# The weight tiles of a cross-attention kernel moved by 32 bytes

## What is computed

```python
text_p  = x   @ W_text  + b_text          # 512 -> 512
audio_p = ctx @ W_audio + b_audio         # 384 -> 512
Q = layer_norm(text_p, g1, beta1)
K = layer_norm(audio_p, g2, beta2)
alpha = softmax(Q @ K.T / sqrt(512))      # 256 x 256 in each sequence
h = (alpha @ audio_p) @ W_out + b_out
out = layer_norm(h + x, g_out, beta_out)
```

## Time and profile before

| | |
|---|---|
| median of 3 runs | 1266.14 us (1266.1 to 1266.36) |
| profiled execution: its time | 1266.2 us |
| profiled execution: its span, first to last instruction | 1264.4 us |
| TensorE matmuls | 1251.3 us busy, 6648 of them |
| TensorE weight loads | 1067.3 us busy |
| VectorE, ScalarE, GpSimd | 1079.9, 1054.0, 548.7 us busy |
| TensorE's clock over the span | 0.999 of full speed |

### The profile page before, as it was taken

One profiled execution on the slowest core, in us unless ns is written; L12 is line 12 of the kernel. 1 busy time (PEld: TensorE's weight loads), 2 busy tenths in 40 slices (PEclk: granted clock), 3 DMA queues, 4 the chain that ended last, 5 costly groups with the idle time before them and its releaser, 6 DMA issues.

```text
span 1264.4 us, 22572 instructions
## 1 busy us (share of the span) xinstructions
PE 1251.3 (99%) x6648; PEld 1067.3 (84%) x6648; DVE 1079.9 (85%) x1735; ACT 1054.0 (83%) x1791; POOL 548.7 (43%) x545
## 2 busy tenths in 40 slices
PE   8999999999999999999999999999999999999997
PEld 6688888888888888888888888888888888888886
DVE  6788888898888888888988888888888888889888
ACT  7788888888888888888888888988888888888884
POOL 0122555433554434554435544335544345543356
PEclk9999999999999999999999999999999999999999
DMA  7356876777866767866768767678667688667693
GB/s 258 92 153 177 245 227 169 200 185 215 241 213 174 196 187 233 234 192 179 187 203 243 227 172 197 185 220 240 206 177 190 192 238 230 187 185 188 207 236 106
DMA packets 96645, 252.49 MB, mean 200 GB/s; under 512 B 9456, under 2 KB 25328, under 8 KB 88688
## 3 DMA queue, kind: packets, MB, share of 16 engines
q1 hardware_dynamic: 75408, 187.22, 42.2%
q0 software_dynamic: 21216, 65.02, 28.6%
HBM read 137.38 MB, written 49.81 MB: 148 GB/s over the span
## 4 chain that ended last, share of the span: by engine, by line
PE 97%; DVE 1%; ACT 1%; issue 0%; DMA 0%; SPq 0%; DVEq 0%; ACTq 0%
PE wide L372 9%; PE wide L376 9%; PE wide L375 9%; PE score L300 7%; PE score L301 7%; PE score L302 7%; PE wide L302 7%; PE wide L300 7%; PE wide L301 7%; PE wide L430 7%; PE wide L429 7%; PE wide L428 7%; PE turn L301 1%; PE turn L302 1%; PE turn L300 1%; PE turn L382 1%
## 5 line engine op out<-in xcount | busy, mean ns | idle before, releaser
L1275 POOL TENSOR_TENSOR y_rows<-y_rows,betao_row 128x512 f32<-128x512 f32 x120 | 166.7, 1389 | 339.3 <-ACT y_rows L649 226.3
L372 PE MATMUL wide<-xT_hi,wt_hi 128*128 128x512 f32 x496 | 195.8, 395 | 0.3 <-DVE xT_lo L860 0.3
L376 PE MATMUL wide<-xT_hi,wt_lo 128*128 128x512 f32 x496 | 195.9, 395 | 0.0
L375 PE MATMUL wide<-xT_lo,wt_hi 128*128 128x512 f32 x496 | 195.8, 395 | 0.0
L608 ACT ACTIVATE squares<-wide,bac_col 128x512 f32<-128x512 f32 x128 | 88.4, 690 | 78.8 <-PE wide L302 77.1
L302 PE MATMUL wide<-cT_hi,wa_lo 128*128 128x512 f32 x372 | 146.8, 395 | 0.0
L300 PE MATMUL wide<-cT_hi,wa_hi 128*128 128x512 f32 x372 | 146.8, 395 | 0.0
L430 PE MATMUL wide<-wao_hi,pcT_lo 128*128 128x512 f32 x372 | 146.7, 394 | 0.0
L428 PE MATMUL wide<-wao_hi,pcT_hi 128*128 128x512 f32 x372 | 146.6, 394 | 0.0
L301 PE MATMUL wide<-cT_lo,wa_hi 128*128 128x512 f32 x372 | 146.6, 394 | 0.0
L300 PE MATMUL score<-kT_hi,qT_hi 128*128 128x256 f32 x512 | 145.4, 284 | 1.1 <-DVE qT_lo L936 1.1
(11 more groups left out here) (170 smaller groups left out, 3554.0 us busy)
## 6 DMA issues: line engine op xcount, KB each, us to landing
xT_in<-in_xT SPq DMA_DIRECT2D x31, 1024.0 KB, 8.6
y_rows<-in_x_rows SPq DMA_DIRECT2D x124, 256.0 KB, 4.1
y_rows<-bao_row POOLq DMA_DIRECT2D x31, 1024.0 KB, 9.4
out<-y_rows SPq DMA_DIRECT2D x124, 256.0 KB, 3.4
xT_lo<-xT_in POOLq DMA_DIRECT2D x30, 1024.0 KB, 9.0
c_kept<-in_c_rows SPq DMA_DIRECT2D x32, 768.0 KB, 6.9
cT_in<-in_cT SPq DMA_DIRECT2D x31, 768.0 KB, 8.8
p_out<-probs SPq DMA_DIRECT2D x31, 512.0 KB, 4.7
```

The costliest lines, as they stand in the source:

```text
L372: nc.tensor.matmul(wide[h][:], wt_hi[:, d, cols], xT_hi[:, d, :], start=(d == 0), stop=False)
L375: nc.tensor.matmul(wide[h][:], wt_hi[:, d, cols], xT_lo[:, d, :], start=False, stop=False)
L376: done = nc.tensor.matmul(wide[h][:], wt_lo[:, d, cols], xT_hi[:, d, :], start=False, stop=(d == DT - 1))
L1275: nc.gpsimd.tensor_tensor(rows, rows, betao_row[:], ALU.add).then_inc(y_ready, 1)
```

## The change

A tile `line_fill` of 8 float32 a partition, 32 bytes, is declared ahead of the weights, and `b_shift`, behind the small tiles, is 32 bytes shorter. Everything declared between the two lies 32 bytes further: the six tiles of weights, the three rows (`bao_row`, `go_row`, `betao_row`), `cols` and the small tiles. What is declared ahead of them and behind them stays where it is. No instruction is added, removed or moved.

```diff
         mean_of = sb("mean_of", [P, P], F32R)
         eps = sb("eps", [P, 1])
 
+        line_fill = sb("line_fill", [P, 8])
+
         wt_hi, wt_lo = sb("wt_hi", [P, DT, H], F32R), sb("wt_lo", [P, DT, H], F32R)
         wa_hi, wa_lo = sb("wa_hi", [P, CT, H], F32R), sb("wa_lo", [P, CT, H], F32R)
         wao_hi, wao_lo = sb("wao_hi", [P, CT, H], F32R), sb("wao_lo", [P, CT, H], F32R)
@@
         b_sum, b_mean = sb("b_sum", [P, 2]), sb("b_mean", [P, 2])
 
-        b_shift = sb("b_shift", [P, 24])
+        b_shift = sb("b_shift", [P, 16])
 
         xT_in, cT_in = sb("xT_in", [P, DT, T * P]), sb("cT_in", [P, CT, T * P])
```

## The result

| | before | after |
|---|---|---|
| median | 1266.12 us | 1271.09 us |
| ratio, 95% interval | | 1.004 [1.003, 1.005] |
| span of the profiled execution | 1264.4 us | 1269.0 us |

The change makes the kernel 5.0 us slower, 0.4%. The forecast was no change, 1266.0 us. First the page and TensorE's waits after the change.

What follows compares the result with a forecast made beforehand. TensorE, busy almost throughout, was taken as the bound: matmuls times pitch. Profiled execution 1266.2 us, with loads 0, streams -0.2 and rest 0, gave 1265.9 to 1266.1, stated as 1266.0; the 8-in-10 range was 1257 to 1274 us.

Steps and rivals of the forecast that it cites:

- What bounds it: Whole kernel: TensorE is 99% busy with no waits from 60 to 1211 us, so time is matmuls times pitch.
- the cost of the stationary operands: 2688 weight loads, phase 0 under streams at phase 32: bounded at 0 to 20 ns each, taken as 0.
- The moving operands: Output stage, 1152 matmuls streaming wao: one 64-byte block fewer each, 0.2 us gain in all, at most 7.7.
- The bound from the context stage: Context streams touch 24 blocks, scores 17; seven more cost 1.5 ns, so 0.2 ns a block.
- Rival A: Output stage: 64-byte blocks feed the stream at about 7.04 ns each; 8.1 us less, 1258 us; chance 0.13.
- Wrong in another way: Sign of other failure: a new mid-kernel TensorE wait, or context and scores changing though their operands keep their addresses; no size.
- The rhythm of seven: Key stage: four matmuls of 0.39 us, then three of 0.40, repeating; read as excess not sitting on one operand.
- Rival C: Load and stream disturb each other when phases differ: 1293 us at 10 ns a load, 1274 at 3; chance 0.15.
- Rival B: Wide matmuls: phase makes the excess over streaming time, in loads and streams; 72.6 us less if all went, 1194; chance 0.05.
- the 18.9 ns: Each wide matmul's pitch beyond the 213.3 ns that 512 columns take at 2.4 GHz; whether addresses touch it was the question.
- the 16.4 ns: Wide matmul pitch, 232.2 ns, less the skill page's 215.8: unexplained, estimated at 63 us over 3840 matmuls, 1203 us.

Runs made afterwards that it cites:

- distance 0: Against the kernel before, weights 32 bytes nearer, data 96 further: stationary and moving addresses equal within 256 bytes; 1250.56 us. Weights 64 nearer, data 64 further: 1250.14 us.

## Why the prediction was wrong

**What bounds it** was right: TensorE's pitch, and nothing else. No wait appeared in the middle, and with the three rows and cols alone on 64 the time was that of before. The measured 1271.09 us also lies within the stated 1257 to 1274; but the forecast was 1266.0 us, with 0.67 on no change and 0.15 on slower.

**The step that failed** is the cost of the stationary operands: "So a load from phase 0 under a stream at phase 32 costs 0 to 20 ns ... I take 0: the output stage's reading is clean". I chose the lower end of a bound that I had rightly drawn, on the reading of a single mean_of load among 37 matmuls, read to 10 ns. The true cost was about 0.04 us / 36 = 1.1 ns a load in the keys and 0.03 / 48 = 0.6 in the queries, some 2 us in all. One load in a stage could not show 1 ns. Nor was it a reading of the change: by the declarations mean_of lay at distance 96 from `sq_parts` and `xT_hi` and at 224 from `wao_hi`, while keys and queries went to 160; that mean_of has phase 0 was the one thing they shared. And in the query stage the load of mean_of had also to wait for `sq_parts`: in the step of the earlier trace rows VectorE finished it at 600.59 us and the load began at 600.64, 0.08 us after the start of the matmul that it should lie behind.

**The moving operands** were the second miss, and the larger: forecast 0.2 us of gain, measured 0.07 us x 31 = 2.2 us of loss. The bound from the context stage answered how many blocks of 64 bytes a stream touches; that question was the wrong one. Rival A, which asked the same question from the other side, forecast 8 us of gain in the output stage and is refuted by the sign. Its agreement at 7.04 ns a block was chance: at distance 0 the streams touch 32 blocks in one kernel and 33 in the other, and the key stage takes 8.19 us in both.

**Context and scores** had no term in the sum, and grew by 0.8 us in 31 steps with operands that kept their addresses. The prediction named this under "Wrong in another way", as a sign "that the pitch hangs on something between tiles"; it is the smallest of the three parts, and no run explains it.

**The rhythm of seven** I read as proof that the excess does not sit on addresses. In that kernel it sits on no single operand, that was right; but the rhythm itself depends on the distance of the two operands. The same view of the changed kernel shows a pattern of three, with some 6 ns more after each L303, and at distance 0 the three members of the key triple have 226.9 to 227.7 ns on average. A rhythm out of step with the program says nothing on whether addresses set its mean.

**Rival C** came nearest, with a chance of 0.15: the position of the stationary operand against the moving one costs time. Its point of decision, 1 ns a load, is about where the keys came out. It counted phases within 64 bytes, where 64 bytes further is 7 us faster; it left the output stage out; its prices of 3 and 10 ns were too high; and that a load and the stream beside it are what meets, as it has it, no run shows. Rival B is refuted as stated (all at phase 0 is no faster), yet its reservation, that the rows could not separate the excess from the common position, was sound: of the 18.9 ns above 213.3, distance 0 removes 4.7.

**On the pages.** The Trainium skill, "TensorE: Matmul & The Clock Gate", section "Step-by-step: what each phase is for", has weights and moving operand on two independent read ports. The pitch of the same matmuls runs from 227.5 to 234.2 ns with the distance of those two operands alone, so here the two operands are not independent in time; whether it is their reads of SBUF that meet, no run shows. "SBUF — State Buffer", section "Door 1: The DMA port swizzle", gives lines of 16 bytes; a step of 16 bytes, from one such line to the next, took the key stage from 8.19 to 8.40 us. The gap of 215.8 ns, which "Back-to-back issue gap" gives for a matmul by itself, is not reached by the wide stages of any kernel; for a stream of loads and matmuls of 512 columns the section gives some 131 ns, far below the 226.8 ns that is the least in the map. So the 16.4 ns of rival B were measured against a figure that the section does not give for such a stream.

**What stays open**: whether the next load meets the running stream or a matmul's own operands meet, and what has a period of 256 bytes. The map is measured; what in the hardware makes it is not shown.

## What to carry to other kernels

In this kernel, where TensorE is busy to the end, the position of the stationary tile against the moving one is worth up to 3% of a wide matmul's pitch in this form of float32; other types and widths were not tried. Where the same holds, try the same position within 256 bytes first (1.2% of this kernel, 1250.14 us, for one line of declarations moved and a filler resized), and measure each position by itself, since neighbouring values do not interpolate. Before relying on one odd instruction as the witness for a thousand others, work out how small an effect per instruction it could show; if that is larger than the effect that decides, keep the bound and not its end.

## What the runs showed that I had not expected

Distance 0 is the best and 16 bytes from it is nearly the worst; of ten distances two are fast (0 and 192), and the others lie within 3 ns. In the kernel at distance 0 the matmul of the mean of squares was itself out of line in the query stage:

```profile
517.22 0.39 PE L372 MATMUL wide<-xT_hi,wt_hi 128*128 128x512 f32 x1
517.44 0.45 PE L382 MATMUL turn<-sq_parts,mean_of 128*128 128x512 f32 x1
517.73 0.39 PE L375 MATMUL wide<-xT_lo,wt_hi 128*128 128x512 f32 x1
```

0.29 us from its start to the next, where 0.23 is the pitch around it: there the query stage loses some 0.06 us a step. This is a wait and no effect of addresses, as the weight load and VectorE's row show:

```profile
517.39 0.19 PEld L382 LDWEIGHTS turn<-sq_parts,mean_of 128*128 128x128 f32 x1 [0.21 <-DVE sq_parts L860]
516.66 0.68 DVE L860 TENSOR_TENSOR sq_parts<-sq_half,sq_parts 64x512 fp32r<-64x512 f32 x1
```

VectorE finishes `sq_parts` at 517.34 us and the load begins at 517.39, only 0.05 us before its matmul. In 28 of 29 middle steps VectorE is done about 0.1 us before that matmul starts, and the next one follows after 286 to 299 ns; in the one step where it is done 0.34 us before, after 227 ns. Before the change it is done 0.21 us before, and no time is lost. So a faster TensorE has run up against VectorE at this one place, some 1.7 us of the kernel's time.

The context stage, none of whose operands changed their distance, takes 4.36 us in some kernels and 4.31 or 4.32 in others. It does so within one kernel too, with the same instructions at the same addresses: before the change 4.32 and 4.36 in turn, with the rows alone on 64 mostly one step of 4.31 and then two of 4.36, with everything on 64 nearly always 4.31. So its time depends on more than addresses; on what, no run shows.
